# 32-head attention on one core: score products over 128 rows, issued last in TensorE's step

## The reference, cut to what matters

```python
q = apply_axial_rope((x @ Wq).reshape(b, n, 32, 8), pos_map)
k, v = jnp.split(ctx @ Wkv, 2, axis=-1)
k = apply_axial_rope(k.reshape(b, ctx_n, 32, 8), ctx_pos_map)
logits = jnp.einsum('bqhd,bkhd->bhqk', q, k) * scale
w = jax.nn.softmax(logits, axis=-1)
attn = jnp.einsum('bhqk,bkhd->bqhd', w, v).reshape(b, n, 256)
return attn @ Wout + bout
```

## Time and profile before

| | |
|---|---|
| median of 3 runs | 2920.95 us (2917.86 to 2922.67) |
| the profiled execution's own time | 2897.66 us |
| its span | 2895.9 us |
| TensorE matmuls busy | 2417.1 us, 83% of the span |
| VectorE / ScalarE / GpSimd busy | 45% / 41% / 34% |
| mean granted TensorE clock | 0.908 of full speed |

### The profile page before, as it was taken

The page is one execution under the profiler, slowest core; times in us unless marked ns, Lnnn a source line. Parts: engine busy times, 40 slices in busy tenths (PEclk is TensorE's granted clock), DMA queues, the critical chain, the costliest instruction groups (busy, mean ns, idle before and its releaser), DMA issues.

```text
span 2895.9 us, 36136 instructions
## 1 busy us (share of the span) xinstructions
PE 2417.1 (83%) x11097; PEld 1532.2 (53%) x11140; DVE 1315.4 (45%) x3349; ACT 1176.4 (41%) x3878; POOL 970.3 (34%) x958
## 2 busy tenths in 40 slices
PE   5999999799999899989999998899948776713663
PEld 4666668466666444446666665466634333303552
DVE  2443444455565333346556553433357756820112
ACT  3444443344455221166665553333326653501111
POOL 3211110100001000034445453245524566446765
PEclk8999999898999999999999999999968787756777
DMA  9920000100000300000000003356651000003776
GB/s 349 350 62 1 1 1 1 40 1 1 1 1 1 108 1 0 0 1 1 1 1 26 7 32 96 116 97 104 100 134 63 8 8 1 8 8 72 154 151 140
DMA packets 159440, 162.77 MB, mean 56 GB/s; under 512 B 26932, under 2 KB 151108, under 8 KB 158485
## 3 DMA queue, kind: packets, MB, share of 16 engines
q1 hardware_dynamic: 127124, 119.64, 13.7%
q0 software_dynamic: 32128, 40.82, 7.8%
HBM read 81.35 MB, written 79.10 MB: 55 GB/s over the span
## 4 chain that ended last, share of the span: by engine, by line
PE 64%; DVE 11%; issue 8%; ACT 5%; DMA 5%; POOL 5%; SPq 1%; POOLq 0%; DVEq 0%; ACTq 0%
PE ps L134 54%; DMA moe_sum<-work,weights 3%; PE ps L1115 2%; ACT work L953 2%; PE ps L550 2%; POOL slots L2846 2%; POOL work L2923 1%; PE ps L224 1%; DVE xn L250 1%; PE ps L578 1%; PE ps L411 1%; ACT work L635 1%; PE ps L2284 1%; PE ps L2299 1%; DVE bn L236 1%
## 5 line engine op out<-in xcount | busy, mean ns | idle before, releaser
L134 PE MATMUL ps<-work,weights 128*128 128x512 f32 (+5 forms) x1920 | 754.0, 533 | 37.4 <-issue 27.2
L134 PE MATMUL ps<-xn_T,weights 128*128 128x512 f32 (+5 forms) x1392 | 546.3, 530 | 23.2 <-DMA weights<-in_L_ffn_Wd 6.9
L134 PE MATMUL ps<-weights,work 128*128 128x126 f32 (+5 forms) x2496 | 536.5, 348 | 6.2 <-DVE weights L435 4.7
L134 PEld LDWEIGHTS ps<-work,weights 128*128 128x128 f32 (+4 forms) x1932 | 312.4, 198 | 238.2 <-issue 181.9
L134 PEld LDWEIGHTS ps<-weights,work 128*128 128x128 f32 (+2 forms) x2496 | 358.7, 197 | 41.2 <-issue 7.4
L134 PEld LDWEIGHTS ps<-xn_T,weights 128*128 128x128 f32 (+3 forms) x1392 | 232.0, 192 | 201.7 <-issue 170.9
L720 POOL TENSOR_TENSOR work<-work,rinv 128x512 f32<-128x512 f32 x128 | 133.4, 1042 | 310.3 <-DVE rinv L670 284.2
L1184 ACT ACTIVATE work<-ps,n_negm 128x128 f32<-128x128 f32 x512 | 146.2, 371 | 123.4 <-DVE n_negm L1211 123.2
L953 ACT ACTIVATE work<-ps,n_negm 128x112 f32<-128x112 f32 (+1 forms) x512 | 152.7, 348 | 101.0 <-DVE n_negm L981 100.8
L256 POOL TENSOR_TENSOR rstd<-var,neg_half 128x4 f32<-128x4 f32 x32 | 35.2, 1101 | 432.2 <-DVE var L241 432.2
L635 ACT ACTIVATE work<-ps,negm,rq 128x128 f32<-128x128 f32 x256 | 113.8, 454 | 136.8 <-DVE negm L688 136.8
(11 more groups left out here) (311 smaller groups left out, 3762.3 us busy)
## 6 DMA issues: line engine op xcount, KB each, us to landing
f_rows<-weights SPq DMA_DIRECT2D x17, 2176.0 KB, 19.1
weights<-in_L_ffn_gate_up_proj SPq DMA_DIRECT2D x16, 768.0 KB, 6.5
work<-f_rows SPq DMA_DIRECT2D x80, 136.0 KB, 2.6
weights<-in_L_ffn_W SPq DMA_DIRECT2D x96, 88.0 KB
weights<-in_L_ffn_down_proj SPq DMA_DIRECT2D x16, 384.0 KB, 7.7
f_sum<-weights SPq DMA_DIRECT2D x2, 2176.0 KB, 15.2
moe_sum<-weights POOLq DMA_DIRECT2D x2, 2176.0 KB, 12.3
weights<-in_L_xattn_Wo SPq DMA_DIRECT2D x2, 2048.0 KB, 12.5
```

The source lines that it names most:

```text
L134: return nc.tensor.matmul(out, lhsT, rhs, start=start, stop=stop, skip_group_check=True)
```

## The change

- TensorE issues S(t) after T(t-3) and V(t-4) of its step, and ahead of the norm's transposes and `beside`; before, it stood first.
- S(t) multiplies all 128 rows of the queries' half with s_kblk, a key block made for this one step, in which the rows of the other three groups are zero.
- GpSimd therefore makes a block for each step: 128 of them in the layer for 32, each of the same 128 x 512 numbers, with the mask of the group (head_sel8) in place of hmask8. Blocks lie in a ring of four, block g is made when S(g-4) is done, and the first three are made ahead.
- The wait for the rotary results is GpSimd's alone; S(t) waits for its block (narrow_kblk_ready).
- The programs of VectorE and ScalarE are as they were. n_on moves to make room.

```diff
+    KB_RING, KB_AHEAD = 4, 3
+    s_kblk = tile(WK, 3072, KB_RING * W).rearrange("p (n h k) -> p n h k", n=KB_RING, h=NB)
+    n_on = tile(WK, 5120, 512).rearrange("p (n d) -> p n d", n=2)
...
         for t in S.steps:
-            if S.new:
-                c, r, b, hf = place(A, t)
-                r0 = r * A.rows
-                if t in A.needs_qk:
-                    done(pe, A.needs_qk[t][0], s, A.needs_qk[t][1])
-                if r == 0:
-                    done(pe, A.kblk_ready, s, c)
-                before = t - 3 if t >= 3 else max(i for i in range(A.n - 3, A.n) if i % 3 == t) - A.n
-                done(pe, A.p_ready, s, before)
-                mm(S_BANKS[t % 3], q_t[r0:r0 + A.rows, hf, b * P:(b + 1) * P],
-                   n_kblk[r0:r0 + A.rows, c % 2, :, :].rearrange("p h k -> p (h k)")).then_inc(A.s_mm.sem, 1)
             u = t - P_LAG
...
                 last.then_inc(A.o_mm.sem, 1)
+            if S.new:
+                c, r, b, hf = place(A, t)
+                done(pe, A.kblk_ready, s, t)
+                before = t - 3 if t >= 3 else max(i for i in range(A.n - 3, A.n) if i % 3 == t) - A.n
+                done(pe, A.p_ready, s, before)
+                mm(S_BANKS[t % 3], q_t[:, hf, b * P:(b + 1) * P],
+                   s_kblk[:, t % KB_RING, :, :].rearrange("p h k -> p (h k)")).then_inc(A.s_mm.sem, 1)
...
+        def key_block(body, g):
+            c, r, b, hf = place(A, g)
             if g in A.needs_qk:
                 done(pool, A.needs_qk[g][0], body, A.needs_qk[g][1])
-            done(pool, A.s_mm, body, max(g - A.per_half - 1, -4))
-            nc.gpsimd.tensor_tensor(out=n_kblk[:, c % 2, :, :],
+            done(pool, A.s_mm, body, g - KB_RING)
+            nc.gpsimd.tensor_tensor(out=s_kblk[:, g % KB_RING, :, :],
                                     in0=k_t[:, hf, b * P:(b + 1) * P].unsqueeze(1).broadcast_to([P, NB, P]),
-                                    in1=head_mask[:].unsqueeze(2).broadcast_to([P, NB, P]),
+                                    in1=head_sel[:, r, :].unsqueeze(2).broadcast_to([P, NB, P]),
                                     op=ALU.mult).then_inc(A.kblk_ready.sem, 1)
...
         for t in S.steps:
-            if S.new and t % A.per_half == 0:
-                c = t // A.per_half + 1
-                if c < A.units:
-                    key_blocks(s, c)
-                elif S.ahead:
-                    key_blocks(s + 1, 0)
+            if S.new and t + KB_AHEAD < A.n:
+                key_block(s, t + KB_AHEAD)
+            elif S.new and S.ahead:
+                key_block(s + 1, t + KB_AHEAD - A.n)
```

More of the change, by code:

```diff
@@ L1060, in __init__ @@
             self.chain = signal("attn_chain", n + TB)
-            self.kblk_ready = signal("narrow_kblk_ready", self.units)
+            self.kblk_ready = signal("narrow_kblk_ready", n)
             self.s_mm = signal("attn_s_mm", n)
@@ L1081, in _build @@
     OUT_AT = O_LAG + 1
-    n_on = tile(WK, 4096, 512).rearrange("p (n d) -> p n d", n=2)
+    KB_RING, KB_AHEAD = 4, 3
+    s_kblk = tile(WK, 3072, KB_RING * W).rearrange("p (n h k) -> p n h k", n=KB_RING, h=NB)
+    n_on = tile(WK, 5120, 512).rearrange("p (n d) -> p n d", n=2)
     def slim_out(blk):
@@ L1224, in slim_dve, with slim_pool @@
             beside(S, t)
-    def slim_pool(pool, S, k_t, head_mask):
+    def slim_pool(pool, S, k_t, head_sel):
         A, s = S.A, S.s
-        def key_blocks(body, c):
-            b, hf = c // KD, c % KD
-            g = c * A.per_half
+        def key_block(body, g):
+            c, r, b, hf = place(A, g)
             if g in A.needs_qk:
                 done(pool, A.needs_qk[g][0], body, A.needs_qk[g][1])
-            done(pool, A.s_mm, body, max(g - A.per_half - 1, -4))
-            nc.gpsimd.tensor_tensor(out=n_kblk[:, c % 2, :, :],
+            done(pool, A.s_mm, body, g - KB_RING)
+            nc.gpsimd.tensor_tensor(out=s_kblk[:, g % KB_RING, :, :],
                                     in0=k_t[:, hf, b * P:(b + 1) * P].unsqueeze(1).broadcast_to([P, NB, P]),
-                                    in1=head_mask[:].unsqueeze(2).broadcast_to([P, NB, P]),
+                                    in1=head_sel[:, r, :].unsqueeze(2).broadcast_to([P, NB, P]),
                                     op=ALU.mult).then_inc(A.kblk_ready.sem, 1)
         if S.new and not S.old:
-            key_blocks(s, 0)
+            for g in range(KB_AHEAD):
+                key_block(s, g)
         for t in S.steps:
-            if S.new and t % A.per_half == 0:
-                c = t // A.per_half + 1
-                if c < A.units:
-                    key_blocks(s, c)
-                elif S.ahead:
-                    key_blocks(s + 1, 0)
+            if S.new and t + KB_AHEAD < A.n:
+                key_block(s, t + KB_AHEAD)
+            elif S.new and S.ahead:
+                key_block(s + 1, t + KB_AHEAD - A.n)
             if S.tail and t - A.tail_t == 2:
@@ L1374, in rope_qk_dve @@
             else:
-                done(dve, L1.kblk_ready, s, (j + 1) * CB * KD - L1.units - 1)
+                done(dve, L1.kblk_ready, s, (j + 1) * CB * L1.groups - L1.n - 1)
         cols = slice(j * CW, (j + 1) * CW)
@@ L3105, in _ @@
         nc.gpsimd.memset(l1_vf, 1.0).then_inc(pool_consts, 1)
-        run_ahead(lambda S: slim_pool(pool, S, l1_k, hmask8), L1, pool)
+        run_ahead(lambda S: slim_pool(pool, S, l1_k, head_sel8), L1, pool)
         pool.wait_ge(rope_ready.sem, rope_ready.value(NS - 1, 3))
```

## The result

The changed kernel takes 3015.57 us (median of 4 runs, 3013.09 to 3018.60) against 2919.40 us for the kernel before on the same chip (2910.28 to 2922.67): a ratio of 1.0337 [1.0317, 1.0357], 96 us slower. The profiled execution's own time is 3017.29 us, its span 3015.5, its mean granted clock 0.902.

The account below looks back on a forecast made before the run. TensorE was taken as the bound, so its waits show in full: +103 us for the order, 0 for the dense product, and +26 for the clock make +129, so 2921 + 129 = 3050 us, range 2995 to 3105.

Parts of the forecast that it names:

- the large term: TensorE in even steps: T(t-2) waits for VectorE's copy behind the maximum of t, 62 x 1.97 us; +103 us after corrections.
- The bound and the order: TensorE, busy 411 of the layer's 421 us, is the bound; S placed last makes T wait, +103 us.
- The late waits: VectorE arriving late at t = 4, 24 and 14: 0.5 us seven times, about 1.3 three times, 7 us.
- The dense product, "I take 0": S on TensorE: a product over 128 rows costs what one over 32 did; 0, with 6 us in the range.
- the long low stretches: TensorE's long stretches at the lower clock in this layer go, since S is dense: -15 us.
- GpSimd's block, 0.22 us on the negative: Key block beside VectorE's negative makes it 0.39 us for 0.17 in every step; counted within the 1.97 us wait.
- No wait of S for its block: Sign expected in the profile: 128 key blocks of 1.04 us, ready well over 4 us early, S never waiting.
- The clock, +26: TensorE's clock in the layer: +41 us for short low stretches after waits, -15 for long ones that go.
- plain waits: TensorE's waits of 1.97 us for the copy: 45% of 53 followed by 3.4 us at half speed, +41 us.
- The reference point: Whole kernel: +129 us added to the median of 2921 us, 23 us above the profiled execution, gives 3050.
- A: Rival, TensorE's clock: waits too short to lower it, only the order counts; +88 us, 3009 us, chance 0.26.
- B: Rival, TensorE's clock: falls after nearly every wait; +178 us, 3099 us, up to 3130, chance 0.16.

Follow-up runs that it names:

- copy_first: Changed kernel with VectorE's copy of t-3 moved ahead of the maximum of t; 2939.49 us, 1.0112 of the kernel before.
- dense_only: Changed kernel with S(t) put back first in the step, 128-row products and a key block per step kept; 2892.70 us, 0.9946 of the kernel before.
- order_only: Kernel before with S(t) moved behind T(t-3) and V(t-4), still 32-row products and 32 key blocks; 3130.41 us, 1.0746 of the kernel before.
- late_blocks: Changed kernel with GpSimd's key block g held until the exponentials of step g-4 are done; 2970.20 us, 1.0211 of the kernel before.

## Why the prediction was right, and where it was not

The forecast was 3050 us, the time 3016: slower, inside the range, 34 us below the likeliest value. The mechanism of the large term was right. Of the others the clock was 13 us too high, the dense product's -31 was missing and +12 was not foreseen, and that these partly cancel is luck. Step by step:

**The bound and the order.** TensorE was the bound, and T's wait for the copy behind the maximum is the cost: copy_first shows that by taking it away. The forecast had +103 us for it, and the trace has 109.9 - 6.9 = +103.0. The agreement to the microsecond is luck, since single terms missed each other. T starts 2.91 us after S (641.73, 644.64) where the forecast has 1.06 + 1.97 = 3.03, mostly because the maximum starts 1.06 us after S's start where it was 1.16; the idle time so seen is 1.89 us. The late waits are longer (up to 4.07 us) than the 0.5 to 1.3 us that I added allow.

**The dense product, "I take 0".** This step failed. I compared the length of records (597 ns against 1.06 to 1.12 us for two) and not the distance from start to start around S in the earlier trace rows: 0.98 before it, 1.06 behind it. Both are longer than the pieces themselves need: dense_only measures 0.89 and 0.86. It is worth 0.34 us in a step that doesn't wait. In the changed kernel a pair of steps keeps TensorE busy 6.52 - 1.95 = 4.57 us where it was 5.06, about 64 x 0.49 = 31 us in the layer. It is worth more than that through the clock: I took -15 us for the long low stretches that it ends, but with S last the same order over 32 rows has a layer 147 us longer (order_only). The Trainium skill (TensorE: Matmul & The Clock Gate, "Why this matters for your kernels") states that a single product over 32 rows takes the same time as one over 128. Here it did not, from start to start, at 32 or 64 rows between products over 128.

**GpSimd's block, 0.22 us on the negative.** Right in place and size (L1209 at 0.38, the wait 1.68 without it), and too small in sum. I counted only the negative, while the longer L1382 (1.49 for 0.69) and the norm's L250 (a mean of 783 ns for 406) stand ahead of the same copy. All of it, with the clock that the longer waits cost, came to 38.6 us, not 13. The Trainium skill (SBUF — State Buffer, "Who interferes with whom") states that a VectorE instruction with two inputs from SBUF contends with GpSimd's reads; L1382 is such a one, and the trace agrees. I should have gone down VectorE's list of instructions by it, not only read the one row where both ran together. No wait of S for its block was found, as forecast.

**The clock, +26.** About half. The clock of the layer, 0.932 after and 0.948 before (rounded in the rows), is some 71 us at 1.2 GHz against some 44: 27 us more, about +13 in time (65 against 37 us in the second pair of traces). The mechanism was not the one I costed. I let 45% of the plain waits be followed by 3.4 us at the lower level. Of 49 plain waits one was (at 651.16; three more only through a longer wait behind them), but all eleven long ones were, eight of them for some 6.8 us; the wait up to 684.09 is one, and the rows from 680 to 690.4 above show its stretch. The Trainium skill (TensorE: Matmul & The Clock Gate, "HAM oscillation — how this bites in real kernels") lets only gaps longer than the plain waits lower the clock. For the changed kernel's plain waits that holds, with one exception. It does not hold for order_only, where 1.68 us was enough in most cases, nor for the five waits of 2.26 to 2.44 us here. What differs in order_only is the product over 32 rows, as far as the counts of the other runs show.

**Not foreseen.** The norm's transposes and the rotary products now wait for VectorE too, 7.9 + 7.4 us in the layer against 2.9: +12. Together: 103 - 31 + 13 + 12 makes 97 us, and the layer grew by 96.2.

**The reference point.** Adding the sum to the median of 2921 rather than to the profiled execution was right: the medians differ by 96, as the layers do. The spans differ by 119.6 because the two profiles caught a different length of the rest (1936.8 and 1962.2).

The rivals: A (the clock stays up, 3009) was nearer the time than my forecast, but not for its reason, since the clock did fall; its sum lacks the same product term. B (falls after nearly every wait) is what order_only did, and the prediction's argument against it, that S over 128 rows does more between the waits, is the one that decided.

## What to carry to other kernels

When an engine's instruction is moved, look at each other engine's program for what still stands in the old order: the order cost 122 us on top of the dense product, and moving the two copies that had kept their place, behind a maximum and behind exponentials, gave 102 of it back. An edit that leaves the amount of work alone can still change how two instructions hand over, so compare starts, not durations. And time background work on GpSimd to begin behind VectorE's sensitive instructions: a single added wait gave 14 to 39 us of the layer in three kernels.

## What the runs showed of the hardware that was not expected

- A float32 product over 32 or 64 rows between products over 128 rows costs 0.31 to 0.34 us a step more than the same over 128. Its weights are loaded at its own start, not 0.11 us ahead, and the hand-over behind it is longer too (1.06 for 0.86). Three steps were measured: 2.53 us (32 rows), 2.53 (64), 2.19 (128).
- The granted clock depends on what runs between the waits: of the plain waits at full clock 21 of 24 were followed by the lower level with S over 32 rows (order_only), 4 of 49 with S over 128, and none of 42 where the waits were as short as in order_only (late_blocks); the layers were at 0.71, 0.93 and 0.97. What in the 32-row product does it was not taken apart.
- A key block on GpSimd beside VectorE makes a 128x4 TENSOR_SCALAR 0.38 in place of 0.17 us, a 128x512 TENSOR_TENSOR with both inputs in SBUF 1.49 in place of 0.69, and L250 0.78 in place of 0.41. The maximum (0.69) and the copy from PSUM (0.68) were not changed.
- A stretch of some 1950 us that no edit touched took 1932 to 1941 us in nine profiles and 1953 to 1962 in five. Spans of single profiles can't be compared without it; the ratio of medians on the same chip came out alike twice (1.0337, 1.0338).
